# Mamba section of a macaron block: six places for GpSimd's products with C, VectorE's gate product one scan later, TensorE's skip term one place later

## The chip, the cores and the metric

The kernel runs on one NeuronCore of one Trainium2 chip. The metric is the device time of one execution in microseconds (us). Engines are called by the profile's names where rows are read: PE is TensorE, DVE is VectorE, ACT is ScalarE, POOL is GpSimd, SP is the engine that queues most DMAs.

## The reference, cut to what matters

The block is `x + 0.5*MoE(norm(x))`, then `x + mamba1(norm(x)) + mamba2(flip(norm(x)))`, then `x + 0.5*MoE(norm(x))` again, on 32 sequences of 256 tokens with 128 features. Only the middle part is touched. One of its two Mamba directions computes, for 256 inner channels and 16 states:

```
xz = x @ in_w.T ; xi, z = split(xz) ; xc = silu(conv(xi) + conv_b)
dt, B, C = split(xc @ xp_w.T)
delta = softplus(dt @ dtp_w.T + dtp_b) ; A = -exp(A_log)
h_t = h_{t-1} * exp(delta_t * A) + (delta_t * xc_t) * B_t      # per channel and state
y_t = sum over the 16 states of h_t * C_t
y = (y + xc * Dp) * silu(z) ; result = y @ out_w.T
```

## The kernel before, in words

The Mamba section works in 32 units: 16 pairs of sequences times 2 directions. Unit u = 2p + r is direction r of pair p; below, an even unit has r = 0 and an odd one r = 1. A unit holds its channels as 128 partitions x 1024 columns (two halves of 512). Nothing is scheduled at run time: each engine runs through a fixed program, in which a unit has places n = 0 to 15, one per state. The tables at the top (`DVE_AT`, `POOL_AT`, `ACT_AT`, `PE_AT`, `SUM_AT`) say at which place an engine slips in work that belongs to the unit before or to the unit after. Half places come behind whole ones.

For state n of the current unit:

- ScalarE makes the decays exp(delta * A) (`decay`, line 1164, three states ahead; for states 3, 9 and 15 `decay_to_bank`, line 1174). The input term du * B is made in one of three ways: VectorE `product` (line 889), GpSimd `product` (line 535, states 3, 9, 15, called at places 0, 4 and 11 by `MUL_AT`), or ScalarE `scale_by_B` (line 1197) and TensorE `turn_back` (line 1522).
- VectorE `scan` runs the recurrence over time (line 917; line 904 for states 3, 9, 15), into one of `R = 4` buffers `hs`.
- GpSimd `times_C` multiplies by C (line 548) into one of 4 buffers `hC`. It waits for the scan, for the row of C (fetched by SP), and for TensorE to have summed the product that lay in its buffer.
- TensorE `sum_states` (line 1547) adds the products into banks 4 and 5, in batches: `SUM_AT` puts states 0, 1, 2 at place 6, states 3 and 4 at place 7, and so on to 14 and 15 at place 18, which is place 2 of the next unit.

`skip` (line 1536, place 4) starts these banks with xc * D; it needs the previous unit's `gate` to have read them. `gate` (line 877) is VectorE's product of the banks with `zs` = silu(z), behind its scan 2 of the next unit. At places 2 to 10 of unit u the next unit is prepared:

- ScalarE `silus` (place 2): a table load and two activations for xc (line 1125), then, behind a wait for `gated`, two for `zs` (line 1130), then another table load (line 1131);
- TensorE `project_z` (place 3) and `project_x` (place 4.5, waits for the first half of `zs`);
- ScalarE `decay(5)`, `scale_by_B` of state 8, in even units `normalise` (line 1103), `decay(6)`, then `split_hi` (place 3.5, line 1135), which writes `BCs`;
- VectorE `split_lo` (behind scan 5, line 864), which reads `BCs`;
- ScalarE `softplus_parts` and `log1pexp`, VectorE `step_size` (behind scan 10, line 870), GpSimd `size_times_input` (line 567, behind its product 9), which makes du of the next unit;
- in even units VectorE `layernorm` (place 2.5, lines 853 and 858) and GpSimd `rstd` (place 1).

The wait in `silus` is there because `zs` of unit u+1 overwrites that of unit u-1, which `gate` reads:

```
if not isinstance(p, int) or 2 * p + r >= 2:
    act.wait_ge(s["gated"], 2 * p + r - 1)
```

GpSimd's program in a unit is thus: C products 0, product 3, C 1, (rstd), C 2, 3, 4, product 9, C 5 to 9, `size_times_input`, C 10, 11, product 15, C 12 to 15.

Of the kernel before, what the change touches and what calls it, by code (L numbers as in the profile page):

```python
# [26 lines left out]
P = 128  # L27
# [12 lines left out]
ACT_NORM = ["xn", "xnT", "xnTrev"]  # L40


DVE_AT = {"stats": 2.5, "gate": 2, "sum": 5.5, "lo": 5.5, "size": 10.5}
POOL_AT = {"rstd": 1, "du": 9}
ACT_AT = {"xn": 3.0, "silus": 2.0, "xnT": 6.5, "hi": 3.5, "BT": 8.0, "parts": 8.5, "ln": 9.0, "gT": 12.0,
    "duT0": 12.5, "duT1": 14.5, "res": 13.5}
PE_AT = {"z": 3.0, "skip": 4, "xdbl": 4.5, "xt": 6.0, "BT": 8.0, "dt": 8.5, "gT": 11.5, "out0": 12.5,
    "out1": 12.5, "duT0": 12.5, "duT1": 14.0}
CONV_AT = {0.0: (0, 3, 1), 0.6: (1, 0, 1), 1.6: (1, 1, 1), 2.0: (1, 2, 2), 14.0: (0, 0, 2), 15.0: (0, 2, 1)}
SUM_AT = {6: (0, 1, 2), 7: (3, 4), 9: (5, 6), 11: (7, 8), 12: (9,), 13: (10,), 15: (11,), 16: (12, 13), 18: (14,  # L50
# [2 lines left out]
EARLY, Y_BUFS = 10, 3  # L53
# [32 lines left out]
def turned_before(u, n):  # L86

    whole, part = divmod(n, NSTATE)
    return (u + whole) * len(TURNED_UNITS) + sum(m < part for m in TURNED_UNITS)
# [28 lines left out]
def wait(eng, sem, value):  # L118

    if isinstance(value, int) and value <= 0:  # L120
        return
    eng.wait_ge(sem, value)


def macaron_kernel(nc, x, gateT, wgT, wuT, wdT, inT, xpT, dtpT, chan, outT, ident, tri, e_rank,
                   e_reset, tile_rank, dest, pad, out):
    T, D = x.shape
    L = 256
    NT = T // P
    NP = T // (2 * L)  # L130
# [4 lines left out]
    C = DI // P  # L135
    NS = 16
# [7 lines left out]
    W = S * L  # L144
    G = 4
    NG = NT // G
# [17 lines left out]
    with ExitStack() as ctx:  # L164
        def sb(name, shape, dt=F32):
            return ctx.enter_context(nc.sbuf_tensor(name, shape, dt))

        def sem(name):
            return ctx.enter_context(nc.semaphore(name))
# [5 lines left out]
        wd_sb = sb("wd_sb", [P, E * IC, D])  # L175
# [8 lines left out]
        id_sb = sb("id_sb", [P, P])  # L184
# [28 lines left out]
        tef = sb("tef", [1, TILES])  # L213
        te = sb("te", [1, TILES], I32)

        R = 4
        CW = C * W
        BUF = R * (3 * CW + W) + 3 * CW
        buf = sb("buf", [P, BUF])
# [3 lines left out]
        with nc.sbuf_tensor("parts", [P, PARTS], F32R) as parts:  # L223
            pass
        over = sb("over", [P, (R + 1) * CW])
        assert PARTS <= (R + 1) * CW

        def carve(at, n):
            return buf[:, at:at + n]
# [41 lines left out]

        dA = over[:, 0:R * CW].rearrange("p (b c s t) -> p b c s t", b=R, c=C, s=S)
        hs = carve(0, R * CW).rearrange("p (b w) -> p b w", b=R)
        hC = carve(R * CW, R * CW).rearrange("p (b w) -> p b w", b=R)
        Cs = carve(2 * R * CW, R * W).rearrange("p (b w) -> p b w", b=R)
        rest = R * (2 * CW + W)
        prod = carve(rest, 2 * CW).rearrange("p (b w) -> p b w", b=2)
# [9 lines left out]
        BT = I1[:, :, :].rearrange("p r (q n) -> p r q n", n=NS)  # L287
# [31 lines left out]
        s = {n: sem(n) for n in names}  # L319
# [3 lines left out]
        def _(sp):  # L323
# [98 lines left out]
            sp.dma_start(wg_sb, wgT).then_inc(s["loaded_w"], DMA)  # L422
            sp.dma_start(wu_sb, wuT).then_inc(s["loaded_w"], DMA)
            sp.wait_ge(s["scaled_done"], turned_before(2 * NP, 0))
            sp.wait_ge(s["comb_done"], NG)
            sp.dma_start(wd_sb[:, :, :], wdT).then_inc(s["loaded_w"], DMA)
            outputs_there(1)
# [14 lines left out]
        def _(pool):  # L442
# [97 lines left out]
            def times_C(p, r, n):  # L540

                u = p * 2 + r
                N = u * NS + n
                b = n % R
                pool.wait_ge(s["scan_done1"], N + 1)
                pool.wait_ge(s[f"C_in{b}"], (u * (NS // R) + n // R + 1) * DMA)
                wait(pool, s["y_done"], N + 1 - R)
                pool.tensor_tensor(hC[:, b, :].rearrange("p (c w) -> p c w", c=C),  # L548
                                   hs[:, b, :].rearrange("p (c w) -> p c w", c=C),
                                   Cs[:, b, :].unsqueeze(1).broadcast_to([P, C, W]),  # L550
                                   ALU.mult).then_inc(s["hC_ready"], 1)
# [27 lines left out]
        def _(dve):  # L579
# [281 lines left out]
            def split_lo(p, r):  # L861

                dve.wait_ge(s["act_pre"], done(ACT_PRE, f"hi{r}", p))
                V.tensor_tensor(BCs[r][LOW:ROWS, :], bank[6][LOW:ROWS, :], BCs[r][LOW:ROWS, :].bitcast(F32),
                                ALU.subtract).then_inc(s["dve_pre"], 1)

            def step_size(p, r):

                dve.wait_ge(s["act_pre"], done(ACT_PRE, f"ln{r}", p))
                V.scalar_tensor_tensor(out=delta[r], in0=pairs[3][:, :], scalar=0.0, in1=tmp, op0=ALU.max,  # L870
                                       op1=ALU.add).then_inc(s["dve_pre"], 1)

            def gate(u, r):
                dve.wait_ge(s["y_done"], (u + 1) * NS)
                wait(dve, s["pe_post"], 2 * u)
                for h in range(S):
                    ins = V.tensor_tensor(gat[:, h * W:(h + 1) * W], bank[4 + h], zs[r][:, h * W:(h + 1) * W], ALU.mult)
                ins.then_inc(s["gated"], 1)
# [41 lines left out]
            def pair(p, first, last):  # L920
                for r in range(2):
# [3 lines left out]
                    for n in range(NS):  # L925
                        scan(p, r, n)
                        if n == DVE_AT["gate"] and not (first and r == 0):
                            gate(u - 1, 1 - r)
                        if prep and n == DVE_AT["lo"]:
                            split_lo(pv, rv)  # L930
# [5 lines left out]
                        if not prep:  # L936
                            continue
                        if n + 0.5 == DVE_AT["lo"]:
                            split_lo(pv, rv)
                        if n + 0.5 == DVE_AT["size"]:  # L940
                            step_size(pv, rv)
                        if r == 0 and not last and n + 0.5 == DVE_AT["stats"]:
                            layernorm(p + 1)
# [325 lines left out]
        def _(pe):  # L1269
# [270 lines left out]
            def sum_states(p, r, n):  # L1540

                N = p * 2 * NS + r * NS + n
                pe.wait_ge(s["hC_ready"], N + 1)
                for q in range(G):
                    for c in range(C):
                        at = (q % 2) * DI + c * P
                        ins = M.matmul(bank[4 + q // 2][:, at:at + P],  # L1547
                                       hC[:, n % R, c * W + q * P:c * W + (q + 1) * P], id_sb[:, :], is_transpose=True,
                                       start=False, stop=(n == NS - 1), skip_group_check=True)
                ins.then_inc(s["y_done"], 1)  # L1550

# [7 lines left out]
            def beside(p, r, at, first, last):  # L1559
# [3 lines left out]
                prep = not (last and r == 1)  # L1563
                if prep and at == PE_AT["duT0"]:
                    turn_du(u + 1, rv, 0)
                if prep and at == PE_AT["duT1"]:
                    turn_du(u + 1, rv, 1)
                if prep and at == PE_AT["BT"]:
                    turn_B(u + 1)
                if at == PE_AT["skip"]:  # L1570
                    skip(p, r)
                if at == PE_AT["gT"] and not (first and r == 0):
                    turn_gated(u - 1, 1 - r)
                if at == PE_AT["out0"] and not (first and r == 0):
                    project_out(u - 1, 1 - r, 0)
# [59 lines left out]
            for n in range(NS, NS + NS // 2):  # L1635
                for m in SUM_AT.get(n, ()):
                    sum_states(NP - 1, 1, m)
# [70 lines left out]
```

## Time and profile before

| | |
|---|---|
| median of 3 runs | 2616.89 us (2616.11 to 2617.27) |
| the profiled execution | 2614.2 us, span 2612.1 us |
| granted clock of TensorE, mean | 0.962 |
| Mamba section's scans | 531.9 to about 2081 us of the span |

Times in rows are from the start of the span. "Idle before" is how long the engine stood still before the instruction, and the name behind `<-` is what ended that. The rows are of one execution.

### The profile page before, as it was taken

Reading aid. Unit: us, or ns where it says so; the run is one execution under the profiler, and the core shown is the slowest. Engines: PE = TensorE matmul, PEld = TensorE weight load, DVE = VectorE, ACT = ScalarE, POOL = GpSimd, SP = SyncE. Lnnn points to the kernel's source line nnn. Section 1 sums busy time; section 2 is a strip of 40 time slices with the busy share of each in tenths; the row PEclk is TensorE's granted clock in tenths of the full one; section 3 lists DMA queues with packets and bytes.
Section 4 is the critical chain, followed back from the end, with each engine's and each line's share of the span. In section 5 each row is a group of like instructions: output and inputs, shape, how many; then the busy total and the mean of one; then the engine's idle time right before and its main releaser. Section 6 shows DMA issues by size and latency. Waiting matters only on the chain.

```text
span 2612.1 us, 48904 instructions
## 1 busy us (share of the span) xinstructions
PE 2227.8 (85%) x15840; PEld 1908.7 (73%) x15840; DVE 2240.6 (86%) x3430; ACT 1895.3 (73%) x3628; POOL 2198.4 (84%) x1402
## 2 busy tenths in 40 slices
PE   4899999668888898888888888888988768999992
PEld 3799999446776777776776766766766647999992
DVE  8766666789999999999999999999999887666666
ACT  4355555389999989999999999999999543555551
POOL 3677777379999999999999999999999936777772
PEclk8999999889999999999999999999999978999996
DMA  7011112533333333333333333333333240111126
GB/s 249 21 48 49 49 50 50 144 94 105 110 103 104 107 106 102 107 107 101 111 101 103 112 100 105 111 107 104 106 107 107 85 161 24 50 49 49 49 49 211
DMA packets 156821, 248.73 MB, mean 95 GB/s; under 512 B 22082, under 2 KB 66018, under 8 KB 155874
## 3 DMA queue, kind: packets, MB, share of 16 engines
q1 hardware_dynamic: 137568, 202.79, 26.1%
q0 software_dynamic: 18208, 37.26, 5.3%
q10 hardware_dynamic: 866, 6.43, 0.6%
q8 instruction: 96, 1.57, 0.2%
q14 instruction: 83, 0.68, 0.1%
HBM read 213.10 MB, written 33.29 MB: 94 GB/s over the span
## 4 chain that ended last, share of the span: by engine, by line
PE 37%; POOL 19%; DVE 15%; issue 14%; ACT 10%; DMA 4%; ACTq 0%; DVEq 0%; POOLq 0%; SPq 0%
PE bank L1351 10%; POOL buf L548 8%; DVE buf L917 7%; PE bank L1547 6%; PE bank L1372 6%; PE bank L1422 4%; POOL token_outputs L497 4%; POOL buf L487 4%; PE bank L1522 3%; PE bank L1332 3%; ACT over L1164 3%; DMA buf<-state_rows 2%; ACT scaled L1197 2%; DVE buf L904 2%; POOL buf L535 2%
## 5 line engine op out<-in xcount | busy, mean ns | idle before, releaser
L548 POOL TENSOR_TENSOR buf<-buf 128x1024 f32<-128x1024 f32 x512 | 1199.9, 2374 | 32.4 <-PE bank L1547 27.0
L917 DVE TENSOR_TENSOR_SCAN buf<-over,bank 128x512 f32<-128x512 f32 x832 | 953.8, 1200 | 4.9 <-PE bank L1522 2.7
L1164 ACT ACTIVATE over<-wgu,negA 128x510 f32<-128x510 f32 x832 | 541.5, 709 | 40.3 <-DVE buf L917 28.8
L1547 PE MATMUL bank<-id_sb,buf 128*128 128x128 f32 x4096 | 515.8, 279 | 6.8 <-POOL buf L548 6.8
L1547 PEld LDWEIGHTS bank<-id_sb,buf 128*128 128x128 f32 x4096 | 478.2, 144 | 57.2 <-issue 46.6
L1351 PE MATMUL bank<-parts 128*128 128x256 f32 x3408 | 447.6, 288 | 17.3 <-DVE buf L767 9.2
L1351 PEld LDWEIGHTS bank<-parts 128*128 128x128 f32 x3408 | 420.7, 193 | 36.7 <-issue 36.7
L1197 ACT ACTIVATE scaled<-wd_sb,I 128x256 f32<-128x256 f32 x896 | 377.3, 497 | 22.6 <-PE bank L1522 22.5
L497 POOL DMA_INDIRECT token_outputs<-buf,slot_out x284 | 299.5, 1055 | 87.9 <-issue 84.0
L487 POOL DMA_INDIRECT buf<-token_rows,slot_token x284 | 284.5, 1002 | 95.4 <-issue 82.5
L1522 PE MATMUL bank<-id_sb,scaled 128*128 128x128 f32 x1792 | 256.0, 280 | 88.3 <-ACT scaled L1197 38.2
L1522 PEld LDWEIGHTS bank<-id_sb,scaled 128*128 128x128 f32 x1792 | 202.8, 142 | 166.8 <-issue 69.3
L1372 PE MATMUL bank<-buf 128*128 128x128 f32 x2272 | 276.3, 275 | 1.1 <-ACT buf L1065 1.1
L1372 PEld LDWEIGHTS bank<-buf 128*128 128x128 f32 x2272 | 265.6, 192 | 1.5 <-issue 1.5
L764 DVE TENSOR_TENSOR parts<-wgu,parts 128x512 fp32r<-128x512 f32 x284 | 183.9, 689 | 88.3 <-ACT parts L1052 53.8
L889 DVE TENSOR_TENSOR bank<-wgu,bank 128x512 f32<-128x512 f32 x384 | 243.5, 680 | 8.8 <-PE bank L1489 6.4
L1422 PE MATMUL bank<-buf 128*128 128x512 f32 (+3 forms) x512 | 248.1, 599 | 1.2 <-ACT buf L1119 1.2
L1065 ACT ACTIVATE buf<-bank 128x256 f32<-128x256 f32 x142 | 54.7, 385 | 266.0 <-DMA token_outputs<-buf,slot_out 169.9
L904 DVE TENSOR_TENSOR_SCAN buf<-bank,buf 128x256 f32<-128x256 f32 x384 | 231.7, 666 | 10.0 <-issue 9.5
L535 POOL TENSOR_TENSOR buf<-wgu,buf 128x1024 f32<-128x1024 f32 x96 | 228.3, 2379 | 0.0
L753 DVE TENSOR_TENSOR parts<-bank,parts 128x256 fp32r<-128x256 f32 x142 | 60.3, 425 | 168.6 <-ACT parts L1042 162.0
L776 DVE TENSOR_TENSOR buf<-buf,bank 128x512 f32<-128x512 f32 x284 | 180.5, 674 | 10.3 <-PE bank L1351 9.2
(170 smaller groups left out, 3061.6 us busy)
## 6 DMA issues: line engine op xcount, KB each, us to landing
buf<-state_rows SPq DMA_DIRECT2D x608, 256.0 KB, 3.2
token_rows<-buf SPq DMA_DIRECT2D x32, 256.0 KB, 2.3
wd_sb<-token_outputs SPq DMA_DIRECT2D x16, 512.0 KB, 4.0
buf<-token_outputs SPq DMA_DIRECT2D x16, 512.0 KB, 4.8
buf<-token_rows,slot_token POOLq DMA_INDIRECT x284, 2.5
token_outputs<-buf,slot_out POOLq DMA_INDIRECT x284
out<-X SPq DMA_DIRECT2D x16, 256.0 KB, 3.6
wgu<-wgT ACTq DMA_DIRECT2D x1, 2048.0 KB, 9.1
```

The lines of the kernel that those rows point to most:

```text
L487: pool.indirect_dma_start(out=xin[:, i % X_BUFS, h, :], out_offset=None, in_=xn_rows[:, :], in_offset=bass.IndirectOffsetOnAxis(ap=slot_to ...
L497: pool.indirect_dma_start(out=yt[:, :], out_offset=bass.IndirectOffsetOnAxis(ap=slot_out[:, i * HT + h:i * HT + h + 1], axis=0), in_=yo[:, ...
L548: pool.tensor_tensor(hC[:, b, :].rearrange("p (c w) -> p c w", c=C), hs[:, b, :].rearrange("p (c w) -> p c w", c=C), Cs[:, b, :].unsqueeze ...
L904: ins = V.tensor_tensor_scan(hs[:, b, w], bank[c][:, q * L:(q + 1) * L], prod[:, turn % 2, w], 0.0, ALU.mult, ALU.add)
L917: V.tensor_tensor_scan(hs[:, b, w], dA[:, b, c, :, :].rearrange("p s t -> p (s t)"), source, 0.0, ALU.mult, ALU.add).then_inc(s[f"scan_don ...
L1164: ins = A.activation(dA[:, n % R, c, :, 1:], delta[r][:, c * W:(c + 1) * W].rearrange("p (s t) -> p s t", s=S)[:, :, 1:], ACT.Exp, scale=n ...
L1197: ins = A.activation(scaled[:, turned_before(u, n) % 2, q, :], duT[:, q, :], ACT.Copy, scale=BT[:, u % 2, q, n:n + 1])
L1351: ins = M.matmul(bk[:, c * TP:(c + 1) * TP], w[:, b, cols], xx[:, b, :], start=(j == 0), stop=(j == 2))
L1372: ins = M.matmul(bank[7][:, h * D:(h + 1) * D], hid[:, b, c * TP + h * P:c * TP + (h + 1) * P], wd_e[:, q, c * D:(c + 1) * D], start=(c == ...
L1422: ins = M.matmul(acc[:, :, j:], tapW[:, r, KW - 1 - j, c * P:(c + 1) * P], xnT[:, r, :, 0:L - j], start=(j == 0), stop=(j == KW - 1), skip ...
L1522: ins = M.transpose(turned_bank(n, c)[:, q * P:(q + 1) * P], scaled[:, turned_before(u, n) % 2, q, c * P:(c + 1) * P], id_sb[:, :])
L1547: ins = M.matmul(bank[4 + q // 2][:, at:at + P], hC[:, n % R, c * W + q * P:c * W + (q + 1) * P], id_sb[:, :], is_transpose=True, start=Fa ...
```

## The change

- GpSimd's products with C get 6 buffers: the four of `hC` and two that lie in `wd_sb`, whose space is free in the Mamba section once the early combination of the first MoE is over. `times_C` waits for the sum of the product six back in place of four back. The six first products wait for that combination, and the reload of `wd_sb` for all sums.
- `gate` moves from behind scan 2 to behind scan 3 of the next unit. In even units `layernorm` (2.5) now stands ahead of it.
- `skip` moves from TensorE's place 4 to place 5, thus behind `project_x` and behind `turn_back` of state 6.

```
-DVE_AT = {"stats": 2.5, "gate": 2, "sum": 5.5, "lo": 5.5, "size": 10.5}
+DVE_AT = {"stats": 2.5, "gate": 3, "sum": 5.5, "lo": 5.5, "size": 10.5}
-PE_AT = {"z": 3.0, "skip": 4, "xdbl": 4.5, ...
+PE_AT = {"z": 3.0, "skip": 5, "xdbl": 4.5, ...
-        R = 4
+        R, C_BUFS = 4, 6
+        hC_more = wd_sb[:, 0:2 * CW // D, :].rearrange("p (b k) d -> p b (k d)", b=2)
+        def weighted(N):
+            k = N % C_BUFS
+            return hC[:, k, :] if k < R else hC_more[:, k - R, :]
...
             sp.wait_ge(s["scaled_done"], turned_before(2 * NP, 0))
+            sp.wait_ge(s["y_done"], 2 * NP * NS)
             sp.wait_ge(s["comb_done"], NG)
...
-                wait(pool, s["y_done"], N + 1 - R)
-                pool.tensor_tensor(hC[:, b, :].rearrange("p (c w) -> p c w", c=C),
+                wait(pool, s["y_done"], N + 1 - C_BUFS)
+                if N < C_BUFS:
+                    pool.wait_ge(s["comb_done"], NG)
+                pool.tensor_tensor(weighted(N).rearrange("p (c w) -> p c w", c=C),
...
-                                       hC[:, n % R, c * W + q * P:c * W + (q + 1) * P], id_sb[:, :], is_transpose=True,
+                                       weighted(N)[:, c * W + q * P:c * W + (q + 1) * P], id_sb[:, :], is_transpose=True,
```

## Rows read from the trace of the kernel before

**Rows 1.** A stretch of Mamba: busy PE, PEld, DVE, ACT, POOL; clock, DMA share, GB/s.

```profile
1000.00:1300.00 300.00, 262.76 (x1764) 213.13 (x1763) 292.62 (x361) 275.50 (x503) 295.47 (x137) 0.98 0.36 107
```

**Rows 2.** GpSimd's groups of instructions, 532 to 2086 us: busy, mean, idle before.

```profile
L548 POOL TENSOR_TENSOR buf<-buf 128x1024 f32<-128x1024 f32 x512 | 1199.9, 2374 | 32.4 <-PE bank L1547 27.0 <-DVE buf L917 5.2
```

**Rows 3.** VectorE's groups of instructions, 532 to 2086 us.

```profile
L877 DVE TENSOR_TENSOR buf<-bank,wgu 128x512 f32<-128x512 f32 x62 | 39.9, 686 | 17.9 <-PE bank L1547 17.9
L864 DVE TENSOR_TENSOR BCs<-bank,BCs 40x512 fp32r<-40x512 f32 x31 | 21.5, 695 | 8.8 <-ACT BCs L1135 8.2
```

**Rows 4.** GpSimd's timeline: start, length, instruction, [idle before].

```profile
1248.38 2.40 POOL L567 TENSOR_TENSOR wgu<-wgu 128x1024 f32<-128x1024 f32 x1
1271.70 7.02 POOL L548 TENSOR_TENSOR buf<-buf 128x1024 f32<-128x1024 f32 x3
1279.63 2.38 POOL L548 TENSOR_TENSOR buf<-buf 128x1024 f32<-128x1024 f32 x1 [0.91 <-PE bank L1547]
...
2020.70 2.37 POOL L567 TENSOR_TENSOR wgu<-wgu 128x1024 f32<-128x1024 f32 x1
...
2052.99 2.38 POOL L548 TENSOR_TENSOR buf<-buf 128x1024 f32<-128x1024 f32 x1 [2.01 <-PE bank L1547]
```

**Rows 5.** VectorE's timeline: first preparation, an even unit, an odd unit, last preparation.

```profile
570.34 1.22 DVE L870 SCALAR_TENSOR_TENSOR wgu<-bank,over 128x1024 f32<-128x1024 f32 x1
...
1221.19 1.29 DVE L877 TENSOR_TENSOR buf<-bank,wgu 128x512 f32<-128x512 f32 x2 [0.59 <-PE bank L1547]
1222.40 0.86 DVE L853 BATCH_NORM_STATS2 st<-X 128x6 f32<-128x128 f32 x4
1223.70 2.40 DVE L904 TENSOR_TENSOR_SCAN buf<-bank,buf 128x256 f32<-128x256 f32 x4
1232.17 0.69 DVE L864 TENSOR_TENSOR BCs<-bank,BCs 40x512 fp32r<-40x512 f32 x1 [0.43 <-ACT BCs L1135]
1246.57 1.22 DVE L870 SCALAR_TENSOR_TENSOR wgu<-bank,over 128x1024 f32<-128x1024 f32 x1
...
1264.96 4.55 DVE L917 TENSOR_TENSOR_SCAN buf<-over,bank 128x512 f32<-128x512 f32 x4
1270.10 1.29 DVE L877 TENSOR_TENSOR buf<-bank,wgu 128x512 f32<-128x512 f32 x2 [0.60 <-PE bank L1547]
1271.83 2.44 DVE L904 TENSOR_TENSOR_SCAN buf<-bank,buf 128x256 f32<-128x256 f32 x4 [0.44 <-issue]
1274.18 2.31 DVE L917 TENSOR_TENSOR_SCAN buf<-over,bank 128x512 f32<-128x512 f32 x2
1279.93 0.69 DVE L864 TENSOR_TENSOR BCs<-bank,BCs 40x512 fp32r<-40x512 f32 x1
1294.31 1.22 DVE L870 SCALAR_TENSOR_TENSOR wgu<-bank,over 128x1024 f32<-128x1024 f32 x1
...
1301.45 1.29 DVE L889 TENSOR_TENSOR bank<-wgu,bank 128x512 f32<-128x512 f32 x2 [1.46 <-PE bank L1489]
...
2019.03 1.22 DVE L870 SCALAR_TENSOR_TENSOR wgu<-bank,over 128x1024 f32<-128x1024 f32 x1
```

**Rows 6.** ScalarE's timeline behind the same two gates.

```profile
1223.15 0.60 ACT L1130 ACTIVATE wgu<-bank 128x512 f32<-128x512 f32 x1 [0.70 <-PE bank L1432]
1223.95 0.60 ACT L1130 ACTIVATE wgu<-bank 128x512 f32<-128x512 f32 x1 [0.21 <-PE bank L1432]
...
1231.47 0.67 ACT L1135 ACTIVATE BCs<-bank,id_sb 104x512 fp32r<-104x512 f32 x1
...
1272.06 0.60 ACT L1130 ACTIVATE wgu<-bank 128x512 f32<-128x512 f32 x1 [0.70 <-PE bank L1432]
...
1273.48 1.28 ACT L1131 ACT_TABLE_LOAD   x1
1274.77 1.34 ACT L1164 ACTIVATE over<-wgu,negA 128x510 f32<-128x510 f32 x2
...
1278.84 0.68 ACT L1135 ACTIVATE BCs<-bank,id_sb 104x512 fp32r<-104x512 f32 x1
```

More of the change, by code:

```diff
@@ L46 @@
     "duT0": 12.5, "duT1": 14.5, "res": 13.5}
-PE_AT = {"z": 3.0, "skip": 4, "xdbl": 4.5, "xt": 6.0, "BT": 8.0, "dt": 8.5, "gT": 11.5, "out0": 12.5,
+PE_AT = {"z": 3.0, "skip": 5, "xdbl": 4.5, "xt": 6.0, "BT": 8.0, "dt": 8.5, "gT": 11.5, "out0": 12.5,
     "out1": 12.5, "duT0": 12.5, "duT1": 14.0}
@@ L274, in macaron_kernel @@
         hC = carve(R * CW, R * CW).rearrange("p (b w) -> p b w", b=R)
+        hC_more = wd_sb[:, 0:2 * CW // D, :].rearrange("p (b k) d -> p b (k d)", b=2)
+        assert C_BUFS == R + 2 and 2 * CW // D <= Y_BUFS * G * 2
+        def weighted(N):
+            k = N % C_BUFS
+            return hC[:, k, :] if k < R else hC_more[:, k - R, :]
         Cs = carve(2 * R * CW, R * W).rearrange("p (b w) -> p b w", b=R)
```

## The prediction

> **What bounds the kernel now.** I began with busy time by stretches. In 300 us of the Mamba section VectorE is busy for 292.6, GpSimd for 295.5, ScalarE for 275.5 [rows 1]. Two engines are nearly full, so a small gap on either counts, and so does anything that makes one wait for the other. Then the groups of both, for the idle time ahead of them. GpSimd's C products wait 27.0 us in all for TensorE's sums [rows 2]; VectorE's gate waits 17.9 us for the sums and its low-part split 8.2 us for ScalarE's `BCs` [rows 3]. Last the timelines of one even and one odd unit, which show in what place each gap stands and how late its releaser is.
>
> The pace: `step_size` starts at 570.34 in unit 0 and at 2019.03 in unit 30, 31 starts in all [rows 5], so 30 units take 1448.7 us, 48.29 each. From one even unit's to the odd unit's (1246.57 to 1294.31) it is 47.74.
>
> GpSimd starts `size_times_input` at 1248.38 and is done with product 3 of the next unit at 1271.70 [rows 4]: ten instructions of one kind of size without a gap, 23.32, or 2.33 each. VectorE's scan 3 needs that product and starts at 1271.83. It is the wait of 0.44 in the odd unit [rows 5], whose releaser the profile doesn't name. From there the order runs scan 3, scans 4 and 5, split, on to `step_size`, which GpSimd's `size_times_input` needs. This is a loop through both engines, and the change puts the gate, with its 1.21 us (1222.40 less 1221.19), inside it.
>
> **The buffers.** GpSimd's wait at product 4 (0.91 in the odd unit [rows 4]) is for the sum of product 0, which TensorE makes at place 6. With six places product 6 waits for it, at least two products and product 9 later, 7 us. So these 27.0 us can go. If GpSimd alone set the pace, that would be the gain. I count nothing for it but the tail, because the next part makes GpSimd wait for VectorE instead. The two added waits cost nothing: the early combinations precede VectorE's first scan, and the reload of `wd_sb` stands behind a wait for the last gate already, which has itself waited for all sums. The new buffers are in the same memory and the instruction's form stays.
>
> **The gate.** Let G be its start. At present it stands behind scan 2 and waits 0.6 for the sums; GpSimd's product 3 isn't needed yet. Scan 2 ends at 1269.42 or so (1264.96 plus four scans at 1.115, the 4.55 of the row less the overlap), and scan 3 can't start before 1271.83. The gate therefore fills a hole that exists in any case. Behind scan 3 it fills none: the hole stays, and the 1.21 us come on top. That is the first cost.
>
> The second is larger. ScalarE's `silus` stops at the wait for `gated` ahead of `zs`. At present the gate is over at 1222.48 and the first `zs` activation starts at 1223.15, released by TensorE [rows 5, 6], so the gate is 0.67 early; in the odd unit likewise (1271.39 against 1272.06). Now it ends a scan and more later, and ScalarE stands at that wait. Behind it in its queue are the second half of `zs`, the table load, decay 5, the scaling for state 8, in even units the four normalisations, decay 6 and `BCs`. All that is busy work, so the delay goes straight through to VectorE's split:
>
> - odd: `zs` at 1272.06, `BCs` done at 1278.84 + 0.68 = 1279.52, so 7.46, less the 0.21 that the second `zs` half waits for TensorE (the even unit's row; TensorE will be done by then): 7.25.
> - even: 1223.15 to 1231.47 + 0.67 = 1232.14, 8.99 less 0.21: 8.78.
> - gate start to `zs`: its 1.29 and 0.03 of release, 1.32. `BCs` to split: 0.03.
>
> G to the start of the split is then 8.60 odd, 10.13 even. VectorE's own work in between is 1.21 for the gate and, from scan 4 to the split in the odd unit, 1279.93 less 1274.18 = 5.75 [rows 5]: 6.96. So VectorE stands for 1.64 in an odd unit and 3.17 in an even one, where it now waits 0 and 0.43.
>
> ScalarE's length rests on the table load: it starts at 1273.48 and decay 5 at 1274.77 [rows 6], 1.29 in all. The Trainium skill, "ScalarE: Activation LUTs", section What ACT_TABLE_LOAD costs, has 1.28 us for the load and another 1.38 us to drain, 2.66 us for a switch. By that each unit's chain would be some 1.4 us longer, an estimate from that page; the row shows no such gap here, and the row decides.
>
> **The loop added up.** From `step_size` start:
>
> - to scan 3: `size_times_input` can start 1.25 later (1.22 and 0.03; now 1.81 and 1.66 in the traced units), then 1271.83 less 1248.38 = 23.45: 24.70. VectorE itself would be there sooner: 1246.57 to the end of scan 2 is 22.85, plus 1.30 for `layernorm` in even units (1222.40 to 1223.70), 24.15. So GpSimd decides in both.
> - scan 3 to G: 1274.18 less 1271.83 = 2.35.
> - G to split: 8.60 or 10.13.
> - split to `step_size`: 1246.57 less 1232.17 = 14.40 (odd: 14.38).
>
> An odd unit takes 24.70 + 2.35 + 8.60 + 14.38 = 50.03, an even one 51.58; a pair 101.6 where it is now 96.58. GpSimd has 20 or so products at 2.33 in a unit, 47 to 49 us, and keeps up; its idle time moves to `size_times_input`, where it waits for `step_size` some 2 us in each unit.
>
> Fifteen pairs lie between the first and last `step_size`: 1524.2 us, 75.5 more. Behind the last there is no `zs` and no split, and GpSimd sets the end: it gains the 2.01 of its last wait [rows 4] and 0.4 of the late `size_times_input` (2019.03 + 1.25 against 2020.70). The part outside is unchanged. Sum: 2614.2 + 75.5 - 2.4 = 2687.3 for the profiled execution. That one lies 2.7 below the median of the runs shown, so I forecast 2690.
>
> **The skip term.** Two ways to read it, both near nothing. It takes some 1.9 us on TensorE. Moved behind `project_x`, it lets that start earlier, but `project_x` will wait for the late `zs` and still be done over 2 us ahead of `split_hi`, which ScalarE reaches later. At place 5 it stands ahead of the sums of states 0 to 2 and of the spread of B for product 7. From G: `zs` half 1.92, `project_x` to about 4.7, turn of state 6 to 5.6, skip to 7.5, three sums to 10.2, and the spread is wanted at 10.5 in the odd unit. Just hidden. Were it not, up to 1.5 us a unit could show; the only such wait that the traced pair has is 1.46 at another product, 13 [rows 5]. I take nothing, and 16 us (1.1 in each pair) as the upper end: 2706.
>
> **The rivals.**
>
> - *Only ScalarE's delay counts.* If GpSimd's ten instructions in the loop turned out to be slack (VectorE waits nothing for product 3), the odd unit would be 22.85 + 2.35 + 8.60 + 14.38 = 48.18 and the even one 24.15 + 2.35 + 10.13 + 14.40 = 51.03: 2.63 a pair more than now, 39.5 in all, less 2.4, which makes 2654. For it: the loop's wait is small today, 0.44. Against it: that is with the gate in the hole.
> - *Faster.* GpSimd's waits go and nothing else becomes late: a pair takes 96.58 less the two waits at product 4 (27.0 over 29 times, 0.93 each), so some 27 us in all, 2590. This needs `BCs` no later than 6.96 behind G. The rows have 8.60 and 10.13; it decides from the point at which ScalarE's wait for `gated` isn't the last, thus only if ScalarE reached `zs` 3 us later than the gate's end in any case. It is there before it today.
> - *TensorE's queue.* The skip behind the turn makes sums or spreads late: 2706, as above, or a little more if it meets the even unit too.
> - *Nothing.* The saved 27 us and a smaller delay cancel.
>
> **How the numbers follow.** Forecast 0.72, only ScalarE's delay 0.10, TensorE's queue 0.09, faster 0.06, nothing 0.03. The forecast's own spread is 8 us, from a latency of some 0.25 at each of two hand-overs in 30 units. The range goes from the lesser stall to the queue: 2652 to 2708. Measurement tells 0.2% (5 us) from no change. Faster by more than that 0.06, within 0.03, slower 0.91.
>
> **What the changed profile would show.** ScalarE's line 1130 no longer waits for TensorE's line 1432 but for VectorE's line 877, 3 us each unit, over 90 in all. VectorE's line 864 waits for ScalarE's line 1135 at every unit, 1.6 and 3.2 in turn, about 72 in all; its line 904 has a wait of 1.9 and 0.6 in turn at scan 3; line 877 waits no more for line 1547. GpSimd's line 548 waits no more for line 1547, and line 567 waits about 2 for line 870. The distance of `step_size` starts is 50.0 and 51.6. The prediction is wrong if `BCs` comes without a wait of VectorE (then ScalarE wasn't held), or if scan 3 waits for nothing (then the lesser rival).

## The result, and the profile after

The changed kernel takes 2695.86 us (median of 5 runs, 2691.28 to 2705.74), the kernel before, on the same chip, 2616.11 (2613.38 to 2617.27). The ratio is 1.0311 (95%: 1.0291 to 1.033): 3.1% slower. The profiled execution took 2691.28, with a span of 2689.2 against 2612.1, 77.1 more. The forecast was 2690.

The lines named here stand 11 further down in the changed kernel than in the one before: the gate is 888, the low-part split 875, scan 3 is line 915 (with scans 9 and 15), the other scans 928, `step_size` 881, `zs` 1141, `BCs` 1146, the C product 559, `size_times_input` 578, `project_x` 1465. The spreads are line 1500: one matmul each, by which TensorE lays a row of B over all partitions for a product of VectorE.

VectorE's groups over the Mamba section of the kernel after (busy, mean, idle before with its releasers):

```profile
L928 DVE TENSOR_TENSOR_SCAN buf<-over,bank 128x512 f32<-128x512 f32 x832 | 954.7, 1199 | 19.6 <-ACT over L1175 16.9
L900 DVE TENSOR_TENSOR bank<-wgu,bank 128x512 f32<-128x512 f32 x382 | 242.8, 681 | 16.6 <-PE bank L1500 16.6
L915 DVE TENSOR_TENSOR_SCAN buf<-bank,buf 128x256 f32<-128x256 f32 x384 | 231.6, 665 | 33.3 <-issue 33.3
L888 DVE TENSOR_TENSOR buf<-bank,wgu 128x512 f32<-128x512 f32 x62 | 39.1, 672 | 0.0
L875 DVE TENSOR_TENSOR BCs<-bank,BCs 40x512 fp32r<-40x512 f32 x31 | 21.5, 695 | 54.5 <-ACT BCs L1146 54.5
```

The same view of the kernel before, for the three groups that [rows 3] doesn't hold:

```profile
L917 DVE TENSOR_TENSOR_SCAN buf<-over,bank 128x512 f32<-128x512 f32 x832 | 953.8, 1200 | 4.9 <-PE bank L1522 2.7 <-issue 0.2
L889 DVE TENSOR_TENSOR bank<-wgu,bank 128x512 f32<-128x512 f32 x382 | 242.2, 680 | 6.4 <-PE bank L1489 6.4
L904 DVE TENSOR_TENSOR_SCAN buf<-bank,buf 128x256 f32<-128x256 f32 x384 | 231.7, 666 | 10.0 <-issue 9.5
```

Busy times and means are the same to 0.4% (the gate's is 0.8 us shorter): no instruction of VectorE became slower. Its idle time grew: 19.6 + 16.6 + 33.3 + 54.5 = 124.0, where before had 4.9 + 6.4 + 10.0, and from [rows 3] 17.9 and 8.8, 48.0 in all. The difference, 76.0, is the whole growth of the span but for 1.1. So the change can be read as a balance of VectorE's waits. The gate's wait went (-17.9); those of the split (+45.7), of scans 3, 9 and 15 (+23.3), of the other scans (+14.7) and of the products (+10.2) grew.

The timeline of VectorE in the first preparation, an even unit, an odd unit and the last preparation answers to [rows 5]:

```profile
569.96 1.21 DVE L881 SCALAR_TENSOR_TENSOR wgu<-bank,over 128x1024 f32<-128x1024 f32 x1
...
1230.22 1.22 DVE L881 SCALAR_TENSOR_TENSOR wgu<-bank,over 128x1024 f32<-128x1024 f32 x1
...
1254.96 2.43 DVE L915 TENSOR_TENSOR_SCAN buf<-bank,buf 128x256 f32<-128x256 f32 x4 [0.75 <-issue]
1257.31 1.26 DVE L888 TENSOR_TENSOR buf<-bank,wgu 128x512 f32<-128x512 f32 x2
...
1262.43 2.33 DVE L928 TENSOR_TENSOR_SCAN buf<-over,bank 128x512 f32<-128x512 f32 x2 [0.43 <-ACT over L1175]
1267.31 0.69 DVE L875 TENSOR_TENSOR BCs<-bank,BCs 40x512 fp32r<-40x512 f32 x1 [2.55 <-ACT BCs L1146]
...
1281.64 1.22 DVE L881 SCALAR_TENSOR_TENSOR wgu<-bank,over 128x1024 f32<-128x1024 f32 x1
...
1306.37 2.43 DVE L915 TENSOR_TENSOR_SCAN buf<-bank,buf 128x256 f32<-128x256 f32 x4 [2.03 <-issue]
1308.72 1.26 DVE L888 TENSOR_TENSOR buf<-bank,wgu 128x512 f32<-128x512 f32 x2
...
1313.83 2.33 DVE L928 TENSOR_TENSOR_SCAN buf<-over,bank 128x512 f32<-128x512 f32 x2 [0.43 <-ACT over L1175]
1317.18 0.69 DVE L875 TENSOR_TENSOR BCs<-bank,BCs 40x512 fp32r<-40x512 f32 x1 [1.01 <-ACT BCs L1146]
...
1320.69 1.29 DVE L900 TENSOR_TENSOR bank<-wgu,bank 128x512 f32<-128x512 f32 x2 [0.45 <-PE bank L1500]
...
1332.08 1.22 DVE L881 SCALAR_TENSOR_TENSOR wgu<-bank,over 128x1024 f32<-128x1024 f32 x1
...
2096.44 1.22 DVE L881 SCALAR_TENSOR_TENSOR wgu<-bank,over 128x1024 f32<-128x1024 f32 x1
```

The gate stands behind scan 3 and waits for nothing; behind it a scan waits 0.43, for a decay, and the split 2.55 and 1.01. From gate to split it is 10.00 (1267.31 less 1257.31) in the even unit and 8.46 in the odd. From `step_size` to `step_size` the even unit takes 51.42 (1230.22 to 1281.64) and the odd one 50.44 (to 1332.08). The 30 units between the first and the last `step_size` take 1526.5.

ScalarE's `zs` in the waits of the kernel after (engine, line, releaser: us in total, times, longest), then ScalarE's timeline, then GpSimd's:

```profile
ACT wgu L1141 <- DVE buf L888: 103.9, 30, 3.8
```

```profile
1258.61 1.09 ACT L1141 ACTIVATE wgu<-bank 128x512 f32<-128x512 f32 x2 [3.83 <-DVE buf L888]
1259.71 1.28 ACT L1142 ACT_TABLE_LOAD   x1
1261.01 1.33 ACT L1175 ACTIVATE over<-wgu,negA 128x510 f32<-128x510 f32 x2
```

```profile
1282.94 2.38 POOL L578 TENSOR_TENSOR wgu<-wgu 128x1024 f32<-128x1024 f32 x1 [2.04 <-DVE wgu L881]
```

In [rows 6] the first `zs` waited 0.70 for TensorE. Now both halves run as one row behind 3.83 us of standing still, released by the gate: that is the hold. GpSimd, nearly full before [rows 1], now stands 2.04 for `step_size`.

Last, TensorE in both kernels, at the place that the skip term left. After, then before:

```profile
1254.25 1.99 PE L1443 MATMUL bank<-in_sb,buf 128*128 128x256 f32 x8
1259.85 0.47 PE L1500 MATMUL bank<-BCs,sel 104*128 104x512 f32 x1 [3.60 <-DVE buf L928]
1260.15 3.37 PE L1465 MATMUL bank<-wgu,xp_sb 128*104 128x512 f32 x4
```

```profile
1221.92 1.99 PE L1432 MATMUL bank<-in_sb,buf 128*128 128x256 f32 x8
1223.75 1.95 PE L1536 MATMUL bank<-in_sb,wgu 128*128 128x128 f32 x16
1227.36 0.47 PE L1489 MATMUL bank<-BCs,sel 104*128 104x512 f32 x1 [1.66 <-DVE buf L917]
1227.67 1.88 PE L1454 MATMUL bank<-wgu,xp_sb 128*104 128x512 f32 x4
```

The same four matmuls of `project_x` take 3.37 (3.57 in the odd unit) instead of 1.88, behind an idle of 3.60 instead of 1.66. The traced pair is on the slow side: of 27 units of the kernel after between 600 and 2000 us, 20 have them at 2.58 to 3.62 and 7 at 1.88. The windows of the gap and of what follows it say why; the third number from the right is the granted clock. After, then before:

```profile
1256.20:1259.80 3.60, 0.04 (x1) 0.00 (x0) 3.60 (x7) 1.18 (x3) 3.29 (x6) 1.00 0.25 81
1259.80:1263.30 3.50, 3.46 (x5) 1.26 (x6) 3.07 (x4) 3.49 (x6) 3.50 (x2) 0.59 0.36 110
```

```profile
1225.70:1227.40 1.70, 0.04 (x1) 0.07 (x1) 1.70 (x3) 1.69 (x4) 1.54 (x4) 1.00 0.37 127
1227.40:1229.40 2.00, 2.00 (x6) 0.87 (x7) 2.00 (x3) 2.00 (x6) 2.00 (x1) 1.00 0.63 147
```

The clock is 1.00 (2.4 GHz) in the gap and 0.59 on average over `project_x`, so mostly at the lower level, 1.2 GHz. The prediction's sum had no such term. How much of the loss it carries is one question for the experiments.

### The profile page after: what moved, and what is told of

Its sections match the earlier page's. It is cut to its first block, busy times and chain, and to the rows that moved or that the text cites. A ratio compares the mean times of both kernels' runs of the same rounds, so it can differ in the third digit from the quotient of the medians.

```text
span 2689.2 us, 48904 instructions
## 1 busy us (share of the span) xinstructions
PE 2268.6 (84%) x15840; PEld 1932.3 (72%) x15840; DVE 2243.7 (83%) x3430; ACT 1892.0 (70%) x3628; POOL 2198.4 (82%) x1402
## 4 chain that ended last, share of the span: by engine, by line
PE 27%; POOL 21%; DVE 21%; issue 18%; ACT 7%; DMA 4%; DVEq 0%; ACTq 0%; POOLq 0%; SPq 0%
PE bank L1362 9%; DVE buf L928 9%; POOL buf L559 7%; PE bank L1383 5%; DVE buf L915 5%; POOL token_outputs L506 4%; POOL wd_sb L559 4%; POOL buf L496 4%; DMA buf<-state_rows 3%; PE bank L1558 3%; PE bank L1343 3%; POOL buf L544 2%; DVE bank L900 2%; ACT over L1175 2%; ACT scaled L1208 2%
## 5 line engine op out<-in xcount | busy, mean ns | idle before, releaser
L928 DVE TENSOR_TENSOR_SCAN buf<-over,bank 128x512 f32<-128x512 f32 x832 | 954.7, 1199 | 19.6 <-ACT over L1175 16.9
L559 POOL TENSOR_TENSOR buf<-buf 128x1024 f32<-128x1024 f32 x342 | 802.7, 2369 | 33.5 <-DVE buf L928 32.2
L559 POOL TENSOR_TENSOR wd_sb<-buf 128x1024 f32<-128x1024 f32 x170 | 400.4, 2369 | 12.8 <-DVE buf L928 12.3
L1558 PE MATMUL bank<-id_sb,buf 128*128 128x128 f32 x2736 | 352.4, 280 | 3.2 <-POOL buf L559 3.2
L1558 PEld LDWEIGHTS bank<-id_sb,buf 128*128 128x128 f32 x2736 | 323.0, 145 | 35.3 <-issue 30.4
L1533 PEld LDWEIGHTS bank<-id_sb,scaled 128*128 128x128 f32 x1792 | 214.2, 148 | 173.1 <-issue 76.6
L1533 PE MATMUL bank<-id_sb,scaled 128*128 128x128 f32 x1792 | 268.7, 289 | 82.4 <-DVE bank L900 35.2
L900 DVE TENSOR_TENSOR bank<-wgu,bank 128x512 f32<-128x512 f32 x384 | 244.1, 681 | 19.1 <-PE bank L1500 16.6
L915 DVE TENSOR_TENSOR_SCAN buf<-bank,buf 128x256 f32<-128x256 f32 x384 | 231.6, 665 | 33.3 <-issue 33.3
L1500 PE MATMUL bank<-BCs,sel 104*128 104x512 f32 x192 | 96.2, 526 | 130.6 <-DVE buf L928 130.4
```

Source lines behind the costliest of these rows:

```text
L559: pool.tensor_tensor(weighted(N).rearrange("p (c w) -> p c w", c=C), hs[:, b, :].rearrange("p (c w) -> p c w", c=C), Cs[:, b, :].unsqueeze ...
L900: V.tensor_tensor(bank[c], du[r][:, c * W:(c + 1) * W], B_bank[vector_before(0, n) % 2], ALU.mult).then_inc(s["mul_done"], 1)
L915: ins = V.tensor_tensor_scan(hs[:, b, w], bank[c][:, q * L:(q + 1) * L], prod[:, turn % 2, w], 0.0, ALU.mult, ALU.add)
L928: V.tensor_tensor_scan(hs[:, b, w], dA[:, b, c, :, :].rearrange("p s t -> p (s t)"), source, 0.0, ALU.mult, ALU.add).then_inc(s[f"scan_don ...
L1533: ins = M.transpose(turned_bank(n, c)[:, q * P:(q + 1) * P], scaled[:, turned_before(u, n) % 2, q, c * P:(c + 1) * P], id_sb[:, :])
L1558: ins = M.matmul(bank[4 + q // 2][:, at:at + P], weighted(N)[:, c * W + q * P:c * W + (q + 1) * P], id_sb[:, :], is_transpose=True, start= ...
```

## The experiments

Two theories. **A**, the prediction's: the late gate holds ScalarE at `zs`, `BCs` comes late, and the gate's own time stands in the loop through GpSimd; the skip term costs next to nothing. **B**: the late skip costs as much or more, by TensorE. Each ratio is to the kernel before on the same chip, and so is each loss or gain in us: the median less that of before beside it, by which the whole change costs 80. The kernel before had medians of 2614.38 beside the first four, 2612.86 beside the next four, 2614.13 beside the three after them, and 2615.8 beside the last.

### The three parts one by one

**gate_only**: the kernel before with this edit.

```diff
-DVE_AT = {"stats": 2.5, "gate": 2, "sum": 5.5, "lo": 5.5, "size": 10.5}
+DVE_AT = {"stats": 2.5, "gate": 3, "sum": 5.5, "lo": 5.5, "size": 10.5}
```

> Only the gate moves behind scan 3; four buffers and the skip at place 4 as before. Theory (ScalarE's zs waits for the late gate, and the gate's 1.21 us lie in the loop through GpSimd's product 3): all of the loss is here already. Pair of units 101.6 plus up to 0.3, since GpSimd's product 4 now waits some 2.5 for the sums but has that much time before step_size. 2690 to 2700. Waits of VectorE's split for BCs 1.0 and 2.5 to 3.2 in turn. Rival (six buffers or the skip's place cause a good part): under 2670.

Measured: 2708.58, ratio 1.0363 (1.0347 to 1.0379). ScalarE's `zs` waits 119.0 for the gate. Beside it GpSimd's C products wait for the sums, 81.3 in all: with four places the late gate delays the sums of the next unit, and these block GpSimd. Line 904 (scans 3, 9 and 15) waits 52.1 and the products 52.4, but the split only 27.7. So the time is some 9 us above the expectation, and its composition is another: less is lost at the split than expected, more behind it.

**skip_only**: the kernel before with this edit.

```diff
-PE_AT = {"z": 3.0, "skip": 4, "xdbl": 4.5, ...
+PE_AT = {"z": 3.0, "skip": 5, "xdbl": 4.5, ...
```

> Only the skip moves to place 5; four buffers, gate behind scan 2. Theory: the skip's 1.9 us now lie between the turn of state 6 and the sums of states 0 to 2, so the sum of product 0 comes 1.3 (even) and 1.7 (odd) later, GpSimd's product 4 waits 1.5 and 2.6 for it, and as GpSimd is full, size_times_input and product 3 come later by as much: 3 us a pair, 45 in all, 2655 to 2665. Rival (TensorE has room, the skip's place is worth nothing): 2616, within 5.

Measured: 2717.56, ratio 1.0391 (1.0375 to 1.0407), 103 us slower, and far above both expectations. TensorE's timeline of skip_only, and then VectorE's behind it:

```profile
1271.96 0.47 PE L1489 MATMUL bank<-BCs,sel 104*128 104x512 f32 x1 [3.44 <-DVE buf L917]
1272.27 3.58 PE L1454 MATMUL bank<-wgu,xp_sb 128*104 128x512 f32 x4
```

```profile
1276.77 0.69 DVE L864 TENSOR_TENSOR BCs<-bank,BCs 40x512 fp32r<-40x512 f32 x1 [0.42 <-ACT BCs L1135]
...
1281.84 1.29 DVE L889 TENSOR_TENSOR bank<-wgu,bank 128x512 f32<-128x512 f32 x2 [2.01 <-PE bank L1489]
```

The split waits its old 0.42, but product 7 waits 2.01 for its spread. TensorE does `project_x` in 3.58 instead of 1.88, then the turn of state 6, the skip, four transposes of the normalised input and three sums, and only then the spread. VectorE's wait for spreads is 73.1 in all (6.4 before), and GpSimd waits 60.6 for sums.

**buffers_only**: the changed kernel with the gate at 2 and the skip at 4 again.

> Only the six buffers; gate behind scan 2, skip at place 4. Theory: GpSimd's 27 us of waits for the sums go, but the loop shortens only by the lateness of size_times_input (0.4 to 0.6 in each unit) before VectorE's own order decides; with 2.4 at the end 11 to 17 us, 2600 to 2606. Rival (GpSimd alone sets the pace): all 27 us, 2590. Rival (other memory or a worse meeting of transfers): 2616 or more.

Measured: 2604.51 (2603.87 to 2606.15), ratio 0.9962 (0.9949 to 0.9976). This is as expected (2600 to 2606), and faster than both kernels: clear of the noise, but by 0.4% only. GpSimd no longer waits for sums (27.0 in [rows 2]). It waits 14.2 for `step_size` instead, so 10 us come through and not 27. The gate's wait stays: 19.3 in the window from 532 to 2160 us, where before has 21.6.

The three parts alone give +94, +103 and -10. Their sum is 187; together they give 80. So the parts overlap, and each has to be seen with the buffers in place.

### The gate and the skip on six buffers

**buffers_gate** and **buffers_skip** are buffers_only with one of the two edits above.

> Six buffers and the gate behind scan 3; skip at place 4 as before. The skip now stands behind the late gate in TensorE's queue, and TensorE idles 2.8 us ahead of it, so it runs at the lower clock (3.64 in place of 1.95 in the run of the gate alone) and product 5 waits about 2. Against that, project_x behind it runs at full clock. Theory: within 6 of the changed kernel, 2690 to 2700, and 10 to 18 below the gate alone, since the sums no longer hold GpSimd. Rival (the skip at place 5 is what costs most of the change): below 2660.

Measured: 2687.52, ratio 1.0282 (1.0265 to 1.03). The gate alone, on six buffers, gives nearly the whole loss: +75, so 85 over buffers_only, beside 90 for gate and skip together. That is 3 us below the expected range. TensorE isn't undisturbed here: its skip at place 4 stands behind the late gate and waits 60.4 us for it between 600 and 2000 us, its matmuls take 337 ns on average (275 before), and VectorE waits 30.2 for spreads, more than the 16.6 of the kernel after. So the 5 us between the two kernels can't be read as the price of the late skip alone: one disturbance of TensorE stands here in place of another.

> Six buffers and the skip at place 5, gate behind scan 2. Theory: with nothing between project_z and the spread for product 5, TensorE idles 3.4 us, its clock falls to one half, project_x takes 3.4 to 3.6 in place of 1.9, and the skip's own 1.9 now stands ahead of the sums, so product 7 waits 1.7 to 2.0 in each unit: 2655 to 2665. Rival (only GpSimd's wait for the late sums made the skip's place dear, and six buffers cure it): 2604 to 2610.

Measured: 2648.22, ratio 1.0133 (1.0116 to 1.015). The skip alone gives +35, 45 over buffers_only. Its `project_x` matmuls take 775 ns on average between 600 and 2000 us, 592 in buffers_only, and VectorE waits 42.3 for spreads, where it is 6.5 in buffers_only. The time lies in the expected range. So of the 103 in skip_only 45 remain; the rest came with the four buffers. It isn't every unit that is slow: behind TensorE's gap of 3.44 or more, in the even units, the four `project_x` matmuls take 2.79 to 3.53; behind the 2.16 to 2.39 of the odd ones they take 1.88, with one exception.

**skip_twice** asks whether it is the empty place or the late skip. It is buffers_skip with the skip term made at place 4 as well. The second one starts the accumulation anew, so TensorE does the same 16 matmuls twice.

```diff
-                if at == PE_AT["skip"]:
+                if at in (4, PE_AT["skip"]):
```

> The kernel with six buffers, gate behind scan 2, and the skip term made twice: at place 4, where it only fills TensorE's gap, and again at place 5, whose result counts. It has 1.9 us more work for TensorE in each unit. Theory (the lower clock behind the gap is a good part of the cost): project_x takes 1.9 again and the time falls by 20 to 30 against the kernel with the skip at place 5 alone, to 2630 to 2640; what stays is the second skip ahead of the sums. Rival (the clock plays no part, the order is all): no faster than with the skip at place 5 alone, or slower by its extra work.

Measured: 2623.5, ratio 1.0038 (1.0024 to 1.0053): 25 us faster than buffers_skip, with 1.9 us more work for TensorE in each unit. The fall is the expected one, the time itself lies 6 us under the range given. The group of `project_x` between 600 and 2000 us, in buffers_skip and then in skip_twice:

```profile
L1465 PE MATMUL bank<-wgu,xp_sb 128*104 128x512 f32 x116 | 74.1, 775 | 0.0
```

```profile
L1465 PE MATMUL bank<-wgu,xp_sb 128*104 128x512 f32 x116 | 54.5, 592 | 0.0
```

With the gap filled, the mean is that of before (591). So of the skip's 45 us, 25 go with the gap and the lower clock behind it. The other 20 I put down to the later place of the skip itself, since VectorE still waits 17.4 for spreads, 10.9 more than in buffers_only; that share is argued, not tested.

### The hold of ScalarE, taken away and put in alone

**zs_three**: the changed kernel with a third `zs` buffer, so that `zs` waits for the gate of a unit earlier.

```diff
-                    act.wait_ge(s["gated"], 2 * p + r - 1)
+                    act.wait_ge(s["gated"], 2 * p + r - 2)
-                    step(A.activation(zs[r][:, c * W:(c + 1) * W], bank[6 + c], ACT.Silu))
+                    step(A.activation(zs[(2 * p + r) % 3][:, c * W:(c + 1) * W], bank[6 + c], ACT.Silu))
```

> The changed kernel with a third zs buffer, so that ScalarE waits for the gate before last, which is long over; gate still behind scan 3, skip at 5, six buffers. Theory: ScalarE's hold is the larger part of the loss and goes; what stays is the gate's 1.21 in the loop through product 3. Odd unit 48.4, even 48.9, pair 97.3: 2620 to 2630, and the split waits 0 and 0.5. Rival (the order on VectorE is all, ScalarE's hold is a symptom): stays near 2696. Rival (the hold is all): 2600 or less.

Measured: 2683.11, ratio 1.0266 (1.0251 to 1.0282). At +69 that is only 11 us better than the whole change, and 53 to 63 above what A expected. The hold is gone and the split's wait falls from 54.5 to 15.4. But something else takes its place, in VectorE's groups of zs_three:

```profile
L901 DVE TENSOR_TENSOR bank<-wgu,bank 128x512 f32<-128x512 f32 x382 | 243.2, 683 | 57.4 <-PE bank L1503 57.4
```

```profile
1254.83 0.77 PE L1503 MATMUL bank<-BCs,sel 104*128 104x512 f32 x1 [3.61 <-DVE buf L929]
1255.39 3.62 PE L1468 MATMUL bank<-wgu,xp_sb 128*104 128x512 f32 x4
```

VectorE now waits 57.4 for spreads, where it was 16.6. From the timeline I read the slow `project_x` and the late skip behind it as the cause, hidden until now under the hold. No run has the late gate, the third buffer and the skip at place 4, so that isn't tested. Line 916 (scan 3) still waits 31.8, against 33.3.

**hold_only**: buffers_only in which `zs` waits for scan 3 too. The gate and the skip stay early.

```diff
+                    act.wait_ge(s["scan_done1"], (2 * p + r - 1) * NS + 4)
```

> Six buffers, gate behind scan 2, skip at place 4, and one wait more: ScalarE's zs of the next unit also waits for scan 3, so it starts 2.2 (odd) and 3.0 (even) later than in the kernel before. VectorE's and TensorE's orders are those of the fast kernel. Theory (ScalarE's hold by itself costs, and the third zs buffer won only 13 because TensorE's clock fell and VectorE's wait for product 7 took its place): BCs late by 1.6 and 3.2, 4.4 a pair more, 2660 to 2670. Rival (the hold is worth only those 13): 2604 to 2620.

Measured: 2693.03, ratio 1.0292 (1.0275 to 1.0309). The hold alone, without the late gate or the late skip, costs as much as the whole change: +77, 87 over buffers_only, where that is 90. The expectation, 2660 to 2670, was 23 to 33 too low. ScalarE's `zs` waits 95.0 for scan 3 (103.9 for the gate in the kernel after). VectorE's groups and timeline of hold_only:

```profile
L928 DVE TENSOR_TENSOR_SCAN buf<-over,bank 128x512 f32<-128x512 f32 x832 | 955.3, 1201 | 25.6 <-ACT over L1176 14.9 <-PE bank L1534 7.1 <-POOL buf L559 0.3
L900 DVE TENSOR_TENSOR bank<-wgu,bank 128x512 f32<-128x512 f32 x382 | 242.9, 681 | 24.8 <-PE bank L1501 24.7
L915 DVE TENSOR_TENSOR_SCAN buf<-bank,buf 128x256 f32<-128x256 f32 x380 | 229.0, 665 | 1.8 <-issue 0.5
L888 DVE TENSOR_TENSOR buf<-bank,wgu 128x512 f32<-128x512 f32 x62 | 39.9, 686 | 17.9 <-PE bank L1559 17.9
L875 DVE TENSOR_TENSOR BCs<-bank,BCs 40x512 fp32r<-40x512 f32 x31 | 21.5, 695 | 54.4 <-ACT BCs L1147 54.4
```

```profile
1271.03 0.69 DVE L875 TENSOR_TENSOR BCs<-bank,BCs 40x512 fp32r<-40x512 f32 x1 [2.55 <-ACT BCs L1147]
```

The split waits 54.4, the changed kernel's number, and 2.55 in the even unit, again its number. The rest comes by other ways: scan 3 waits 1.8 instead of 33.3, but the gate 17.9 instead of nothing, and the other scans and the products 50.4, where it is 36.2 after and 13.3 in buffers_only. The five groups sum to 124.5 here and to 124.0 after. The 37 us that scans and products wait longer than in buffers_only are named by their releasers: 14.9 for decays of ScalarE, which buffers_only doesn't list at all, 18.2 more for spreads (24.7 against 6.5), and 4.1 more for turned products (7.1 against 3.0). So the hold reaches VectorE by three ways besides the split, and two of them go through TensorE. That is what the expectation left out.

### GpSimd's loop

**product_early**: the changed kernel with GpSimd's product 3 of the next unit issued two C products earlier, ahead of C 15 instead of behind C 0 of the next unit.

```diff
-MUL_AT = {0: 3, 4: 9, 11: 15}
+MUL_AT = {4: 9, 11: 15}
...
+                        if n == NS - 1 and not (last and r == 1):
+                            product(p + r, 1 - r, POOL_UNITS[0])
...
```

> The changed kernel with GpSimd's product 3 of the next unit moved ahead of its last C product, so that scan 3 finds it ready; nothing else changes. Theory (product 3 is the last to come for scan 3, the loop runs through GpSimd): the waits of 33 us at scan 3 go, 2655 to 2665. Rival (GpSimd's order is slack and some other wait takes their place): stays within 8 of 2696.

Measured: 2645.44, ratio 1.0121 (1.0104 to 1.0138). Scan 3's wait, whose releaser the profile leaves unnamed, falls from 33.3 to 0.2, so it was GpSimd's product. The split still waits 54.5. Scan 3's group in product_early:

```profile
L918 DVE TENSOR_TENSOR_SCAN buf<-bank,buf 128x256 f32<-128x256 f32 x384 | 230.8, 662 | 0.2 <-issue 0.2
```

At +33 it is 47 us better than the whole change and 10 better than expected, more than the 33 of that wait. The wait for spreads falls too, from 16.6 to 5.0: TensorE's gaps are some 2.7 and 1.45 in turn, where the traced pair had 3.60 and 3.59, and the mean of a `project_x` matmul falls from 845 to 666 ns.

**early_zs** is product_early with the third `zs` buffer.

> The changed kernel with both: GpSimd's product 3 of the next unit ahead of its last C product, and the third zs buffer. Theory: the hold through zs (54.5 us of waits for BCs with product 3 early alone) goes, and as VectorE does not stand at scan 3, TensorE's gap stays under the 3.6 us behind which its clock fell, so nothing new takes its place. VectorE's own work is then 94 a pair, GpSimd's 95.2 decides: 2588 to 2600, below the kernel before. The gate behind scan 3 then costs nothing. Rival (each undoing removes the same waits, so they do not add up): 2630 to 2645.

Measured: 2631.81, ratio 1.0066 (1.0054 to 1.0078), near the rival and not the 2588 to 2600 of the first line. The split still waits 32.1 although `zs` waits for no gate. In the traced pair ScalarE goes from the table load to `BCs` without a wait, so I read its own chain as the bound there; that was argued from the timeline, not tested. VectorE waits 27.5 for spreads.

### Looking for more above the buffers alone

**buffers_zs** is buffers_only with the third `zs` buffer, a control: if ScalarE isn't held there, nothing should change.

> Six buffers, third zs buffer, gate behind scan 2, skip at place 4. Theory: with the gate there ScalarE's wait for it is over before TensorE has made z, so a third buffer is worth nothing: within 3 of the kernel with six buffers alone, 2602 to 2608. Rival (the third buffer helps or harms of itself): outside that.

Measured: 2603.47, ratio 0.9962 (0.9948 to 0.9977), the same as buffers_only. The third buffer itself costs and brings nothing.

**norm_late** is buffers_only with the normalisation moved away from the gate.

```diff
-DVE_AT = {"stats": 2.5, ...
+DVE_AT = {"stats": 1.5, ...
-ACT_AT = {"xn": 3.0, ... "xnT": 6.5, ...
+ACT_AT = {"xn": 3.5, ... "xnT": 7.5, ...
-PE_AT = {... "xt": 6.0, ...
+PE_AT = {... "xt": 7.0, ...
```

> Six buffers, gate behind scan 2, skip at 4, and in even units the normalisation's steps moved: VectorE's statistics behind scan 1, ScalarE's four normalisations behind split_hi, TensorE's transposes to place 7 and ScalarE's copies of them to 7.5. Theory: the even unit's BCs come 1.6 earlier and the gate no longer waits 0.6 there, so 0.4 to 0.6 a pair is to be had before GpSimd decides: 2595 to 2602. Rival (the later transposes make a sum or a conversion late): 2606 or more.

Measured: 2605.6 (2604.06 to 2611.25), ratio 0.9974 (0.9962 to 0.9986): no gain over buffers_only, and none of the 2595 to 2602 hoped for. The gate's wait fell from 19.3 to 10.2 and others took it up. The version that beats both kernels stays buffers_only, 0.4% under before.

## Why the prediction was right

**The total.** 2690 against 2695.86. Its sum for the profiled execution was 2687.3, that execution took 2691.28. The loop added up nearly term by term. In the odd unit it put 24.70 from `step_size` to scan 3, 2.35 to the gate, 8.60 to the split and 14.38 to the next `step_size`; the rows give 24.73, 2.35, 8.46 and 14.90, the last with a wait of 0.45 for a spread in it. The even unit took 51.42 for 51.58. The 30 units took 1526.5 for 1524.2. The tail was wrong: it was to gain 2.4, but from the last `step_size` to the end it is 593.1 before (2612.1 less 2019.03) and 592.8 after (2689.2 less 2096.44), a gain of 0.3.

**The gate, second cost (the hold).** Right in mechanism and size. From gate to split it forecast 10.13 and 8.60; 10.00 and 8.46 were traced. It put a stall of 3.17 and 1.64 at the split. The trace has 2.55 and 1.01 there, and 0.43 at the scan ahead of it, for decay 5, in both: 2.98 and 1.44. The forecast of 72 in all for the split is 54.5 there plus the 16.9 that scans wait for decays, 71.4. That ScalarE's hold is enough for a loss of this size was shown by hold_only (87 over buffers_only), though that run's expectation, by the same working, was some 55 to 65: 22 of the 37 us that scans and products wait longer there are for TensorE's spreads and turns, for which the sum has nothing. ScalarE's length was as read: the table load to the next activation takes 1.30 (1259.71 to 1261.01), as in [rows 6]. The Trainium skill, "ScalarE: Activation LUTs", section What ACT_TABLE_LOAD costs, has 2.66 us for a switch; the trace doesn't agree, and by that page each stall would have been some 1.4 longer, an estimate.

**The gate, first cost (the loop through GpSimd).** Right. It gave 1.9 and 0.6 at scan 3; 2.03 and 0.75 were traced (over the section line 915 waits 33.3, where 1.9 and 0.6 in turn make 37.5), and `size_times_input` waits 2.04 for `step_size` where "some 2 us" stood. The odd unit takes 50.44 where 50.03 was forecast. The rival "only ScalarE's delay counts" wants no wait for product 3. There were 33.3 us of it, and they went when the product was issued earlier (product_early). That run won 47 in all; the part above 33 is other waits, the spreads' among them. The two costs don't simply add, however: with the hold and without the gate in the loop (hold_only) the loss is as large as with both.

**The buffers.** Right in that the 27 us don't come through: alone the buffers bring 10 (buffers_only), and in the changed kernel GpSimd's waits for sums go but it waits for `step_size` instead. Beside the other parts they aren't worthless, which the prediction doesn't say: the late gate costs 94 with four buffers and 75 with six, the late skip 103 and 35.

**The skip term, the step that was wrong.** The prediction took nothing for it, with 16 us as the upper end: "Just hidden". It counted at what time TensorE would be done with every instruction at its length of before. It missed that with the skip at place 5 TensorE has nothing left to do between `project_z` and the spread for product 5: in the traced pair it idles 3.60, its clock falls, and `project_x` takes 3.37 to 3.57 instead of 1.88. On six buffers that costs 45 alone, of which 25 are the gap (skip_twice), and with four the late skip costs 103. In the changed kernel it hardly shows: VectorE's wait for spreads is 16.6, 10 more than before, and buffers_gate, without the late skip, costs 75 where the whole costs 80 (there TensorE stands behind the late gate instead). So the sum came out right partly by luck: the term wrongly set at nothing was for the most part hidden, in time that VectorE stood still in any case. With the hold absent, as in zs_three, the forecast by the same working was 53 to 63 too low.

**Open.** What bounds early_zs at the split; what zs_three would take with the skip at place 4; and how much of the wait for spreads and turns in hold_only is TensorE's lower clock and how much its later start.

## What to carry to other kernels

When an instruction is moved, look first for who in another engine's queue waits for it, and count all that is queued behind that wait: here moving an instruction pair of 1.2 us cost 85 on six buffers. Before an instruction is moved out of a place as free, ask what its engine then does there: here the work of TensorE behind the empty place became longer. And test the parts one by one and in pairs, since they hide each other: +94, +103 and -10 alone gave +80 together, and the only part worth keeping was the one that the prediction had counted next to nothing for.

## What the runs showed of the hardware

**TensorE's clock follows short gaps, and unneeded work can pay.** In the traced units, after 3.44 to 3.61 us without a matmul the four of `project_x` took 3.4 to 3.6 instead of 1.88, with a granted clock of 1.00 in the gap and 0.59 on average over them in the kernel after; gaps of 1.66 and 1.46 left them at 1.88. In gate_only the gap was 2.80, and the skip's 16 matmuls behind it took 3.64 instead of 1.95, at a granted clock of 0.53 where the gap ahead of them had 1.00:

```profile
1265.35 3.64 PE L1536 MATMUL bank<-in_sb,wgu 128*128 128x128 f32 x16 [2.80 <-DVE buf L877]
```

It isn't the length of the gap alone. In product_early a gap of 2.70 stood ahead of the first of these two and one of 2.69 ahead of the second; the granted clock was 0.60 over the first and 1.00 over the second:

```profile
845.35 3.04 PE L1468 MATMUL bank<-wgu,xp_sb 128*104 128x512 f32 x4
...
943.64 1.88 PE L1468 MATMUL bank<-wgu,xp_sb 128*104 128x512 f32 x4
```

In the kernel after, a gap of 3.39 once left them at 1.88 (at 1617.55). In hold_only 2.70 was followed by 16 matmuls of the sums in 2.76, which take 1.91 elsewhere in that unit:

```profile
1269.26 0.66 PE L1417 MATMUL bank<-id_sb,xn 128*128 128x128 f32 x4 [2.70 <-ACT xn L1114]
1269.75 2.76 PE L1559 MATMUL bank<-id_sb,buf 128*128 128x128 f32 x16
```

That the clock has two levels, with the lower at half, is what the Trainium skill states in "TensorE: Matmul & The Clock Gate", section What's actually happening; the trace agrees with it, 3.64 to 1.95 being a factor of 1.87. And 16 matmuls more in each unit, whose result isn't used, made a kernel 25 us faster (skip_twice against buffers_skip).

**A wait without a name.** The profile put scan 3's wait down to no instruction ("issue"). It was for GpSimd, as product_early showed: with the product issued earlier it went from 33.3 to 0.2.
